# A fused attention and ternary feed-forward kernel: a new instruction order for every engine, matrix products in 64-column pairs, eleven banks of maxima, V's copy on ScalarE, three PT tiles

## The reference

```python
x = x + _layernorm(attn(_layernorm(x), W_qkv, b_qkv, W_out, b_out))
x = x + _layernorm(ffn(_layernorm(x), weight, alpha, bias))
# attn
qkv = x @ W_qkv + b_qkv
scores = einsum('bkgsd,bktd->bkgst', q, k) / sqrt(8), causal mask, softmax
y = einsum('bkgst,bktd->bkgsd', attn, v) @ W_out + b_out
# ffn: weight is -1, 0 or 1 (threshold 0.7 * mean |weight|), times alpha
out = einsum('bsd,od->bso', input, w_ternary * alpha) + bias
```

## Time and profile before

| | |
|---|---|
| median of three runs | 469.35 us |
| profiled execution, its own time | 467.76 us |
| its span, first to last instruction | 465.9 us |
| PE, PEld busy | 413.6 us (89%), 287.2 us |
| DVE, ACT, POOL busy | 396.6 us (85%), 323.5 us, 297.1 us |
| mean granted TensorE clock | 0.965 |
| DMA packets | 39.50 MB, 36.8% of 16 engines on SP's queue |

### The profile page before, as it was taken

One profiled execution on the slowest core, in us unless ns is written; L12 is line 12 of the kernel. 1 busy time (PEld: TensorE's weight loads), 2 busy tenths in 40 slices (PEclk: granted clock), 3 DMA queues, 4 the chain that ended last, 5 costly groups with the idle time before them and its releaser, 6 DMA issues.

```text
span 465.9 us, 18300 instructions
## 1 busy us (share of the span) xinstructions
PE 413.6 (89%) x6918; PEld 287.2 (62%) x6918; DVE 396.6 (85%) x1307; ACT 323.5 (69%) x577; POOL 297.1 (64%) x552
## 2 busy tenths in 40 slices
PE   1478989999999999999999999999999999998541
PEld 1345657676776667676667677766777766664331
DVE  5768888999999899999999999989999998983441
ACT  1323877777787778788777777777888887767521
POOL 2523335567777677777777677767777776566663
PEclk9998999999999999999999999999999999999755
DMA  6454433354333633363334433363334333501211
GB/s 185 52 51 67 103 85 75 82 108 82 79 74 71 153 75 78 75 159 80 77 77 119 117 74 70 76 158 74 79 79 123 75 74 76 113 28 30 54 41 45
DMA packets 72255, 39.50 MB, mean 85 GB/s; under 512 B 13000, under 2 KB 68008, under 8 KB 72168
## 3 DMA queue, kind: packets, MB, share of 16 engines
q1 hardware_dynamic: 70832, 37.70, 36.8%
q10 hardware_dynamic: 1336, 0.64, 0.5%
HBM read 13.65 MB, written 4.72 MB: 39 GB/s over the span
## 4 chain that ended last, share of the span: by engine, by line
PE 58%; DVE 14%; DMA 8%; issue 7%; POOL 7%; ACT 2%; SPq 2%; ACTq 2%; POOLq 0%; DVEq 0%
PE ps_y L834 13%; PE ps_mx L862 11%; PE ps_st L813 11%; DVE M L651 7%; DMA den<-Y 5%; PE ps_w L890 5%; PE ps_w L927 4%; PE ps_w L918 4%; PE ps_w L928 3%; DVE stats L609 2%; POOL yn L423 2%; PE ps_w L936 2%; PE ps_w L910 2%; PE ps_w L900 2%; DVE Mp L725 1%
## 5 line engine op out<-in xcount | busy, mean ns | idle before, releaser
L651 DVE TENSOR_REDUCE M<-ps_mx 128x2 f32<-128x512 f32 (+3 forms) x448 | 218.6, 529 | 19.6 <-PE ps_mx L862 18.2
L455 ACT ACTIVATE PT<-ps_st 128x1024 f32<-128x1024 f32 (+1 forms) x192 | 168.6, 881 | 23.6 <-PE ps_st L813 12.5
L862 PE MATMUL ps_mx<-KS,QS 112*64 112x64 bf16 (+2 forms) x2560 | 130.6, 225 | 10.7 <-DMA KS<-part 6.4
L862 PEld LDWEIGHTS ps_mx<-KS,QS 112*64 112x64 bf16 x2560 | 88.2, 111 | 55.8 <-issue 26.6
L834 PE MATMUL ps_y<-PT,VB 128*32 128x256 f32 (+3 forms) x2048 | 103.0, 307 | 0.9 <-ACT PT L455 0.9
L813 PE MATMUL ps_st<-QS,KS 114*64 114x256 bf16 (+1 forms) x1024 | 103.7, 304 | 0.0
L395 POOL TENSOR_TENSOR rstd<-vareps,mhalf 128x2 f32<-128x2 f32 x128 | 88.8, 694 | 10.0
L430 POOL TENSOR_TENSOR rest<-QK,part 128x512 f32<-128x512 f32 x32 | 39.3, 1227 | 40.1 <-ACT part L484 40.1
L498 ACT CAST MpT<-ps_w 16x512 bf16<-16x512 f32 x32 | 18.4, 575 | 55.1 <-PE ps_w L900 55.1
L834 PEld LDWEIGHTS ps_y<-PT,VB 128*32 128x32 f32 x2048 | 40.3, 108 | 24.4 <-ACT PT L455 14.6
L813 PEld LDWEIGHTS ps_st<-QS,KS 114*64 114x64 bf16 x1024 | 47.1, 109 | 12.8 <-issue 2.2
(11 more groups left out here) (62 smaller groups left out, 512.8 us busy)
## 6 DMA issues: line engine op xcount, KB each, us to landing
QS<-part SPq DMA_DIRECT2D x192, 64.0 KB
rden<-rec_dram SPq DMA_DIRECT2D x32, 256.0 KB
out<-X SPq DMA_DIRECT2D x8, 512.0 KB, 5.1
X<-in_x SPq DMA_DIRECT2D x7, 512.0 KB, 7.6
KS<-part SPq DMA_DIRECT2D x32, 96.0 KB
KS<-part SPq DMA_DIRECT2D x32, 64.0 KB
KS<-part SPq DMA_DIRECT2D x32, 32.0 KB
QS<-MpT SPq DMA_DIRECT2D x32, 16.0 KB
```

What stands on the lines that cost most here:

```text
L455: nc.scalar.activation(PT[n % 2][:, 0:512 * banks], ps_st[n % 2][:, 0:banks, :].rearrange("p a c -> p (a c)"), ACT.Exp, scale=SCALE).then_ ...
L651: last = nc.vector.tensor_reduce(m[:, pair:pair + pairs, i], ps_mx[n % 2][:, at:at + w].rearrange("p (h t) -> p h t", h=pairs), AX_X, ALU.max)
L862: last = pe.matmul(ps_mx[n % 2][64 * one:64 * one + 64, at:at + w], q[:, h, BL * i:BL * i + BL], k[:, kv, blocks, :], start=True, stop=Tru ...
```

## The change

- **Orders.** The list `step` of each engine is new, and each call names its own lag (`mx(t - 2, 3)`), so that a batch's function can be split over two steps; the lags are no longer the same on all engines. The start of the DVE and PE programs is written out by hand. `take` now waits for the last user of `ps_w` in the program, whatever it is.
- **x.** All groups of x are requested in the first seven steps, one per step. Groups are stored 25 steps after their batch entered SP's program; the last four batches are stored one by one (128 KB each).
- **64-column pairs.** `op`, `ff` and `qk` are written as two products of 64 output rows each instead of one of 128. `turn` writes 32 rows instead of 16 (the maxima's tile Mp has two more parts that hold zeros).
- **Maxima.** Eleven banks: the four first-block pieces `(kv, 0)` have a bank of their own, and every bank is one reduction (11 a batch instead of 14). The cast in `split_max` becomes the maximum of M with itself, two tensor inputs.
- **V.** The mask is put into the weight `wv` (a second copy with zeros in the other half), and V leaves PSUM by a copy on ACT instead of a multiplication on DVE.
- **Buffers.** PT has three tiles instead of two; the small tiles of the layer norms (`mv`, `vareps`, `nmean`, `shift`, `rstd`) have two.

```diff
-BANKS = 10
+BANKS = 11
+TILES = 3
...
 MX_BANKS = [bank for kv in range(0, NKV, 2) for bank in (
-    [(kv, 3)], [(kv + 1, 3)], [(kv, 2), (kv, 0)], [(kv + 1, 2), (kv + 1, 0)], [(kv, 1), (kv + 1, 1)])]
+    [(kv, 3)], [(kv + 1, 3)], [(kv, 2)], [(kv + 1, 2)], [(kv, 1), (kv + 1, 1)])] + [[(kv, 0) for kv in range(NKV)]]
...
-            def load_x(s):
-                if s.t0 % GRP == 2 and s.t0 < B - GRP:
-                    g = s.group(2 - GRP)
+            def load_x(t):
+                g = t + 1
+                if g < B // GRP:
 
                     sp.wait_ge(s_x, g * 16)
                     load(g)
...
+                    if b < B - GRP:
+                        g = b // GRP
+                        sp.dma_start(ov[g], rows(g)).then_inc(s_store, 16)
+                    else:
+                        at = (b - (B - GRP)) * TT
+                        sp.dma_start(ov[B // GRP - 1, :, at:at + TT, :], X[:, TT * b:TT * b + TT, :]).then_inc(s_store, 16)
...
+                act.wait_ge(s_st_ps, CHUNKS * b + n + 1)
+                if b * CHUNKS + n >= TILES:
+                    act.wait_ge(s_pv, CHUNKS * b + n - TILES + 1)
...
+            def take_v(b):
+                if on(b):
+
+                    act.wait_ge(s_v_ps, b + 1)
+                    free(act, b, s_pv, CHUNKS, RING)
+                    nc.scalar.copy(VB[b % RING][:, :, 0:HD],
+                                   ps_w[:, 0:128].rearrange("p (n c) -> p n c", c=HD)).then_inc(s_vb, 1)
...
-                    nc.vector.tensor_copy(Mp[:, 0, :], m).then_inc(s_mp, 1)
-                    dve.wait_ge(s_mp, s.n(TURN, 2, 1))
+                    nc.vector.tensor_tensor(Mp[:, 0, :], m, m, ALU.max).then_inc(s_mp, 1)
+                    dve.wait_ge(s_mp, 2 * b + 1)
...
+            holder = []
+
+            def take(freed, count):
+
+                if holder:
+                    pe.wait_ge(*holder[-1])
+                holder[:] = [(freed, count)]
...
                     for j in range(TT):
                         for lo in range(NLO):
-                            last = pe.matmul(ps_w[:, D * j:D * j + D], y[:, lo, 128 * j:128 * j + 128],
-                                             wo_sb[:, lo, :], start=(lo == 0), stop=(lo == NLO - 1))
+                            for h in (0, 64):
+                                last = pe.matmul(ps_w[h:h + 64, D * j:D * j + D],
+                                                 y[:, lo, 128 * j + h:128 * j + h + 64], wo_sb[:, lo, :],
+                                                 start=(lo == 0), stop=(lo == NLO - 1), skip_group_check=True)
...
-                    pe.matmul(ps_w[:, 0:S], wq_sb[:], xn1T[:], start=True, stop=True)
-                    pe.matmul(ps_w[:, S:2 * S], wk_sb[:], xn1T[:], start=True, stop=True).then_inc(s_qk_ps, 1)
+            def qk(b):
+                if on(b):
+
+                    pe.wait_ge(s_xt, b + 1)
+                    take(s_qk, 2 * b + 2)
+                    for at, w in ((0, wq_sb), (S, wk_sb)):
+                        for h in (0, 64):
+                            last = pe.matmul(ps_w[h:h + 64, at:at + S], w[:, h:h + 64], xn1T[:], start=True,
+                                             stop=True, skip_group_check=True)
+                    last.then_inc(s_qk_ps, 1)
```

More of the change, by code:

```diff
@@ L31, with on @@
 CHUNKS = 6
-BANKS = 10
-NORM, PROJ, SPLIT, MAX, TURN, ATT, DIV, OUT, MID, FFN = range(10)
-STORE = FFN + 1
-STEPS = B + STORE
+BANKS = 11
+TILES = 3
 ON_ACT = (1, 3)
[L39 to L62, removed]
+def on(b):
+    return 0 <= b < B
 ST_CHUNKS = [(lo, mats, banks) for lo in range(NLO) for mats, banks in (
@@ L375, in _ @@
+            for t in range(B + 25):
+                step(t)
+            sp.wait_ge(s_store, 16 * (B // GRP - 1 + GRP))
         @block.gpsimd
@@ L764, in _ @@
-            step(Step(0))
+                if n == 0 and b >= 2:
+                    dve.wait_ge(s_mp, 2 * b - 2)
+                dve.wait_ge(s_mx_ps, BANKS * b + n + 1)
+                kv, i = MX_BANKS[n][0]
+                pairs = 2 * len(MX_BANKS[n])
+                nc.vector.tensor_reduce(
+                    M[b % 2][:].rearrange("p k g i -> p (k g) i")[:, 2 * kv:2 * kv + pairs, i],
+                    ps_mx[(b * BANKS + n) % 2][:, 0:pairs * BL * (i + 1)].rearrange("p (h t) -> p h t", h=pairs), AX_X,
+                    ALU.max).then_inc(s_mx, 1)
@@ L774, in _ @@
-            for t in range(3, STEPS):
-                step(Step(t))
+            moments(4, 0)
+            ternary()
+            spread_x(5)
+            norm_x(3)
+            moments(5, 0)
+            fill(3)
+            spread_x(6)
+            maxima(0, 0)
+            maxima(0, 1)
+            maxima(0, 2)
+            norm_x(4)
+            maxima(0, 3)
+            for t in range(7, B + 14):
+                step(t)
         @block.tensor
@@ new lines, in step @@
+            def step(t):
+                st(t - 4, 4)
+                x1(t)
+                mx(t - 2, 3)
+                st(t - 4, 5)
+                mx(t - 2, 4)
+                qk(t)
+                mx(t - 2, 5)
+                pv(t - 4, 3)
+                pv(t - 4, 4)
+                pv(t - 4, 5)
+                mx(t - 2, 6)
+                op(t - 6)
+                st(t - 3, 0)
+                mx(t - 2, 7)
+                ff(t - 8)
+                st(t - 3, 1)
+                mx(t - 2, 8)
+                mx(t - 2, 9)
+                pv(t - 3, 0)
+                x3(t - 7)
+                mx(t - 2, 10)
+                st(t - 3, 2)
+                st(t - 3, 3)
+                v(t)
+                mx(t - 1, 0)
+                mx(t - 1, 1)
+                pv(t - 3, 1)
+                pv(t - 3, 2)
+                turn(t - 2)
+                mx(t - 1, 2)
@@ L970, in _ @@
             pe.wait_ge(s_early, EARLY)
[L971 to L972 removed]
+            x1(0)
+            qk(0)
+            v(0)
             constants()
[L974 to L979 removed]
+            for t in range(1, B + 8):
+                step(t)
 def kernel(**inputs):
```

734 lines of the change are left out of this document (330 added, 404 removed).

## The result

The changed kernel takes 457.0 us (median of 4 runs, 456.42 to 460.11) where the kernel before takes 469.85 in the same comparison: a ratio of 0.9756, 95% interval [0.9714, 0.9798]. The prediction was 426 us. Direction right, size not: 12.8 us came instead of 43, and the time lies above the range.

What follows compares the result with a forecast made beforehand. TensorE was taken as the bound, VectorE close behind. Start 41.7, batches 0 to 3 30.6, 25 steps of 11.4 (285) and 66 for the rest made 423.3 of span, 425.2 in all, stated as 426 us; range 415 to 446.

Steps and rivals of the forecast that it cites:

- TensorE's work, 12.32 to 11.2: TensorE's steady step: eight fewer output-row switches save 0.80 us, and the 64-column pairs 0.30 us.
- bare weight loads: Rival at `op`, `ff`, `qk`: the pairs' weight loads don't overlap, 0.9 us more, 12.3 a step, 449 us; chance 0.06.
- serial pairs: Rival at `op`, `ff`, `qk`: f32 pairs run one after the other, 13.5 us a step, 478 us; chance 0.05.
- A wait of 0.2 at the shared tile, step 11.4: TensorE at `x1` waits some 0.2 us for ScalarE's copy of `turn`, making the step 11.4 us.
- VectorE "11.78 falls to 10.6, or to 11.1": VectorE's busy us a step, less V, reductions and perhaps 0.5 of the cast; 11.1 if the cast keeps its price.
- TensorE stays the bound: In the steady step, TensorE still sets the time, with VectorE at 93% of the step, where it stood at 96%.
- The first rival: VectorE's norms and cast meet GpSimd operations, TensorE waits for maxima: 0.6 us, 12.0 a step, 441 us; chance 0.23.
- x and SP's queue, 0.29 a step: Loads and most stores of x leave the steady part, taking the 0.29 us a step of excess with them.
- Start, 41.7: First scores of batch 0 come at 41.7 us instead of 44.7, 3 us earlier, bounds 0 and 6.
- End, 66: After batch 28's first scores, 66 us remain instead of 72.0: three steps 1 us shorter each, and 3 at the end.
- the guess of 3 at the end: After the last steps: 2 us from a smaller last store, 1 from the last `op` and `ff` pieces.

Runs made afterwards that it cites:

- e14: e8 with ScalarE copying the feed-forward's transposed rows out of the shared PSUM tile ahead of its norm of the attention output; 445.8 us.
- e12: e8 plus e11's earlier aggregates of the feed-forward norm and e1's shortened row-maximum reductions; 446.6 us.
- e1: Changed kernel with each of the eleven row-maximum reductions reading only the first 64 columns of each piece, leaving out part of the maxima; 448.5 us.
- e9: Kernel before with only the two-tensor cast of the maxima added; 468.8 us, ratio 1.0005.
- e7: Changed kernel with GpSimd's addition of the second residual moved ahead of the first norm's inverse and the remainder; 455.2 us.
- e11: e8 with the feed-forward norm's aggregates taken one step earlier on VectorE, right behind its statistics; 450.5 us.
- e15: Changed kernel with only e14's move on ScalarE, the transposed feed-forward rows copied ahead of the norm; 460.3 us.
- e16: e14 with the feed-forward product one piece of scores later in TensorE's queue; 445.1 us.
- e17: e16 with the values also one bank of maxima later in TensorE's queue; 447.2 us.
- e19: e14 with ScalarE copying the turned maxima ahead of the exponential of the fourth chunk of scores; 448.4 us.
- e8: Changed kernel with VectorE's dependent neighbours apart, GpSimd's second-residual addition earlier, and the step's last reduction ahead of the norm of x; 448.9 us.
- e3: Changed kernel with V's copy back on VectorE, between the first and second reduction; 471.5 us.

## Why the prediction was wrong

The span came out 31.5 us above the forecast: 2.6 at the start, 1.6 in batches 0 to 3, 21.5 in batches 3 to 28, 5.8 at the end. In the 21.5 the step is 12.26 us on average, or 12.35 when quiet, where 11.4 was forecast.

- **TensorE's work, 12.32 to 11.2**: right. Widths change 17 times a step before and 9 after; `op`, `ff` and `qk` came within 0.02 us in e14, and the step of e12 less its waits is 11.1. The rivals of bare weight loads and of serial pairs are out: `op` has 16 records in 0.87 us, where the serial one asked for 1.71, and the bare loads asked for 0.44 on top of 0.86.
- **A wait of 0.2 at the shared tile, step 11.4**: too small. I found `x1`, and called `op` to `ff` and `x3` to `v` covered. They wait 0.15 and 0.16 (0.27 in e12). So TensorE waits 0.4 us a step ahead of products for the shared tile in the changed kernel and 0.6 in e12, where the step is 11.7 with VectorE at 8.7. This is 0.3 of the 0.95 us.
- **VectorE "11.78 falls to 10.6, or to 11.1", and "TensorE stays the bound"**: the step that failed. VectorE's operations were costed at their old prices in a new order. VectorE didn't fall, and it is the bound (e1: with it out of the way the step is 11.96 instead of 12.35). Start to start VectorE went from 12.03 to 12.21 us. The savings came: V 0.20, reductions 0.38, cast 0.38, which leave 11.07. Then the new places took it back: the subtraction 0.47, the norms 0.34, the take of A 0.15, statistics and aggregates of X and A 0.43, less 0.25 at F. More than half of what came back are meetings with GpSimd; the rest are mostly instructions that now directly follow the one whose result they read. This is the other 0.65 us of the step. I had named the danger ("the four norms on VectorE are in the same danger") and put its cost into a rival, at 0.6 us and a chance of 0.23, instead of into the sum.
- **The first rival**, the engines in each other's way with TensorE waiting for `maxima`: right in kind, 12.0 and 441 us were again too little.
- **x and SP's queue, 0.29 a step**: the size is right; the long steps are gone. That the loads and stores did it was not tried alone; the kernel e9, on the old program, still has them (steps of 13.6, 14.2 and 14.3 us at batches 10, 18 and 22). Single long steps, not every four batches, stand in the traces of most later kernels too (13.7 us in e7, 13.9 in e11, 14.3 in e15); what makes those isn't known.
- **Start, 41.7**: 44.3. From the first `mx` to the first `st` 2.4 us were saved (16.5 after, 18.9 before), but the first `mx` comes 2.0 later, at 27.8. Which of the moves ahead of it does that stays open. For batches 0 to 3 the sum took off all 1.1 us of TensorE's saving a step, though the forecast step keeps a wait of 0.2; that is 0.5 us of the 1.6.
- **End, 66**: 71.8, 0.2 under before. Three steps of 1 us less didn't come, and the guess of 3 at the end wasn't borne out.
- **What fixes 11.68 us in e14, e16 and e17**: by the profile's chain the ring through ScalarE between `x3` and `x1`, TensorE, and VectorE behind `op`. It isn't shown by an experiment: e19 shortened its part on ScalarE by 0.16 us and lengthened the rest by 0.27. What fixes the 11.74 of e12, where the reductions are short, stays open.

## What to carry to other kernels

When a change lowers the bound by 9%, cost the engine at 96% in its new order, instruction by instruction against what GpSimd does at that time, before calling it "at 93%". An operation's mean duration belongs to its place, not to its form: the two-tensor cast took 0.16 us in e14 and 0.77 in e9, the subtraction 0.17 in e8 and 0.65 in the changed kernel. One PSUM tile shared by seven products is a lock that passes between queues; sum each taker's delay, and don't move a copy out of it behind other work (14.5 us in e3).

## What I had not expected of the hardware

- The two-tensor form of the 128x32 cast is as exposed to GpSimd's additions as the copy: 770 ns against 817 in one place, 421 against 409 in another, and 162 in e14, where it starts in the last 0.05 us of a GpSimd operation. The Trainium skill, SBUF — State Buffer, Who interferes with whom, names both a copy or cast and an instruction with two SBUF inputs as able to contend with GpSimd, and these rows agree.
- The norms, one SBUF input and scalars, wait too: 689 ns for the first of a pair that starts beside GpSimd's division, 336 for the second, which starts when the division has ended. Beside GpSimd's small 128x2 operation the first takes 339, so not every meeting costs.
- In the changed kernel's trace an instruction on VectorE starts some 83 ns before the end of the one ahead of it, but 34 ns after it if it waits for its result; 0.12 us each time.
